# A decay mixer's first batch: gate products in four other PSUM banks, its silu split in two, and its first four decay tiles ahead of the second batch's preparation

## The chip, the cores and the metric

One NeuronCore of a Trainium2 chip runs the whole program. The time is device microseconds (us) for one execution. A core has TensorE (PE) for matrix products, whose weight loads are listed as PEld, VectorE (DVE), ScalarE (ACT), GpSimd (POOL) and the queues that issue DMAs (SP's and POOL's are used here). The engines run each its own list of instructions in order and wait for each other on semaphores. PE writes only to PSUM, which has eight banks of 128 x 512 float32 numbers; ACT and DVE copy its results from there to the on-chip tiles.

## The reference, cut to what matters

The program computes two layers, each of a mixer and a feed-forward part, on x of shape (8, 512, 256), in float32. The change lies in the mixer of the second layer, the decay mixer:

```python
def _L1_attn_ref(x, W_in, conv_w, ln_gamma, ln_beta, W_xproj, A_param, D, W_out):
    xz = x @ W_in                                  # (8, 512, 256) @ (256, 1024)
    xc, z = jnp.split(xz, 2, axis=-1)
    xc = causal_depthwise_conv(xc, conv_w)         # 4 taps
    xc = jax.nn.silu(xc)
    xc = _layernorm(xc, ln_gamma, ln_beta)
    xp = xc @ W_xproj                              # 33 columns
    delta = jnp.clip(jax.nn.softplus(xp[..., :1]), 1e-06, 10.0)
    Bm = xp[..., 1:1 + n]
    Cm = xp[..., 1 + n:]
    A = -jnp.clip(jax.nn.softplus(A_param), 0.1, 10.0)
    decay = jnp.clip(jnp.exp(delta[..., None] * A[None, None]), 1e-06, 1.0)
    y = xc * jnp.einsum('bsn,bsin->bsi', Bm * Cm, decay)
    y = y + xc * D
    return y * jax.nn.silu(z) @ W_out

x = x + _L1_attn_ref(_layernorm(x, axis=-1), ...)
```

## The kernel before

The program has five stages, A to E, and all engines meet at the end of each. The decay mixer is stage D, the class StageD. It takes eight batches of 512 tokens. For each batch there is a preparation, and then 16 units of decay work; the preparation of the next batch is mixed in among the units of the one before.

The preparation of a batch, by step and engine:

- `stats`, `rstd`, `minus`, `norm`: layer norm of x (DVE, ACT, DVE, ACT; line 2016 is the norm).
- `flip` 0 and 1 (PE, line 1906): transposes, evicted by ACT as `flipped`.
- `lift` c (PE, line 1916): product with 128 columns of W_in. c = 0 to 3 are the convolution's half, c = 4 to 7 the gate's. Each is evicted by ACT (line 2004, `lifted`).
- the convolution: two quarters on PE (`conv` 0 and 1, line 1924, evicted as `conved`), two on DVE (`taps` 2 and 3, lines 2129 and 2132).
- `silu` on ACT: a table load, the silu of the convolution (line 2043), the silu of the gate (line 2046), and a table load back (line 2047).
- `turnx` (PE, line 1931), `stats2`, `rstd2`, `xn` (DVE, line 2145): transposes to tokens by channels, and the second layer norm.
- `back` (PE, line 1939), `xf` (ACT, line 2004 with a bias), `xproj` (PE, line 1948): transposes back, and the product with W_xproj.
- `pj`, `soft`, `clip`, `rep`, `scalars` (DVE line 2154, ACT lines 2062 and 2064, DVE, PE line 1957, DVE line 2169): the step sizes and the products Bm * Cm, spread over the partitions. `zx` on POOL multiplies the gate in.

A unit u of decay work covers eight tokens: `grow` u on ACT (line 2074, one exponential over 128 x 2048), `scale` u on DVE (line 2181, four instructions), and a quarter of `sum` on PE (line 1966), which sums four units into one bank. `wout`, `turnw`, `gate`, `proj` and `acc` follow once for four units.

Once per stage come `decay` on ACT (lines 1997 and 1999) and `bound` on DVE (lines 2103 and 2105), which make A, and `consts` and `spread` on DVE.

One written order sets everything. `order()` walks u from -27 and puts down, for each u, `grow` u+2, `scale` u, `sum`, the output steps, and then the pieces of PLAN for each batch, one entry per u. Batch 0 has its own list, START, and batch 1's PLAN starts at u = -10. Each engine runs its own steps of this one list in that order. PE's products of the preparation share a ring of four banks, 4 to 7 (`self.ring`): a step waits until the use four before it was evicted. Banks 0 and 1 take the sums, 2 the transposed sums and 3 the output product; none of them is in use before the first `sum`.

Of the kernel before, what the change touches and what calls it, by code (L numbers as in the profile page):

```python
# [11 lines left out]
ACT = mybir.ActivationFunctionType  # L12
# [5 lines left out]
LN_EXP = "natural_log_exp_and_others"  # L18
# [7 lines left out]
class Arena:  # L26
    def __init__(self, tensor, start, end):
        self.t, self.at, self.end = tensor, start, end
# [171 lines left out]
def act_rstd(e, m, own, sb):  # L200

    s6, mv, r = sb
    e.activation(r, mv[:, :, 1], ACT.Ln, bias=m.eps5).then_inc(*own.tick())
    e.wait_ge(*own.now())
    return e.activation(r, r, ACT.Exp, scale=-0.5)
# [9 lines left out]
def take_stats(ar):  # L215
    return ar.take([4, 6]), ar.take([4, 2]), ar.take([4])
# [801 lines left out]
class StageB:  # L1018
# [137 lines left out]
    def sp(self, e):  # L1156
# [19 lines left out]
        def load(w):  # L1176
            if w >= 2 * NB:
                return
            if w >= 3:
                e.wait_ge(s["st"], 20 * (w - 2))  # L1180
            for which in range(2):
                e.wait_ge(self.d_scr[which], 16 * (w + 1))
                order = (0, 1, 0, 2, 0, 1, 2, 1) if which else (0, 0, 1, 0, 2, 1, 1, 2)
                for row, part in enumerate(order):
                    e.dma_start(self.stacks[which][w % 3][16 * row:16 * row + 16],
                                self.scr[w % 3 + 3 * which][:, part, :].rearrange("(h j) t -> j h t", j=16)).then_inc(
                                    self.d_stack[which][w % 3], 16)
# [596 lines left out]
class StageD:  # L1784
# [6 lines left out]
    def __init__(self, m, c):  # L1791
        self.m, self.c = m, c
        ar = Arena(m.Z, m.LO, m.HI)
        self.gy = [ar.take([256]) for _ in range(4)]
        self.An = ar.take([4, 512])
        self.wout = ar.take([4, 256])
        self.win = ar.take([2, 1024])
        self.wxp = ar.take([4, 33])
        self.rep = ar.take([4, 128])
        self.pick = ar.take([32])  # L1800
        self.diag = ar.take([2, 4, 128])
        self.dcol = ar.take([4])
        self.sb, self.sb2 = take_stats(ar), take_stats(ar)
        self.nb = ar.take([4])
        self.pj = ar.take([4, 33])
        self.src = ar.take([4, 17])
        self.dl = [ar.take([4, 4]) for _ in range(2)]
        self.bc = [ar.take([16, 4]) for _ in range(2)]
        self.nf = ar.take([2, 512])
        self.xp = ar.take([4, 515])  # L1810
        self.nt = ar.take([4, 256])
        self.xc = ar.take([4, 512])
        self.z = ar.take([4, 512])
        self.xn, self.xf = self.xp[:, :, 3:515], self.xc
        self.zx = [ar.take([4, 512]) for _ in range(2)]
        self.e = [ar.take([4, 512]) for _ in range(10)]
        self.wt = [ar.take([512]) for _ in range(2)]
        self.yf = [ar.take([4, 128]) for _ in range(2)]
        self.wb, self.tb, self.ob = m.banks[0:2], m.banks[2], m.banks[3]
        self.steps = self.order()  # L1820
        self.uses = {}
        for step in self.steps:
            if step[0] in ("flip", "lift", "conv", "turnx", "back", "xproj", "rep"):
                self.uses[step] = len(self.uses)
        self.ring = m.ring(m.banks[4:8], len(self.uses))
        self.d_gy = m.landings(0, 4, 32)
        self.s = {n: m.sem("d_" + n) for n in (
            "d_w", "d_a", "added", "pads", "an", "consts", "moments", "rstd", "nb", "nt", "prod", "conv", "gate", "xc",
            "xn", "bc", "raw", "dl", "sc", "zx", "grow", "scale", "sum", "wt", "tw", "yf", "op", "acc")}

    def use(self, *step):
        return self.uses[step]
# [12 lines left out]
        (("scalars",),))  # L1845


    START = (
        (("stats",), ("consts",)), (("rstd",), ("minus",), ("spread",)), (("norm",), ("decay",)), (("flip", 0), ("flip", 1)),
        (("flipped", 0), ("flipped", 1), ("lift", 2)), (("lifted", 2), ("lift", 3)),  # L1850
        (("lifted", 3), ("taps", 2), ("lift", 0)), (("lifted", 0), ("taps", 3), ("lift", 1)), (("bound",),),
        (("lifted", 1), ("conv", 0)), (("conved", 0), ("conv", 1))) + PLAN[10:]

    def order(self):
        N, out = 16 * NB, []
        for u in range(-27, N + 12):
            b, v = divmod(u, 16)
            if u + 2 in range(N):
                out.append(("grow", u + 2))
            if u in range(N):  # L1860
                out.append(("scale", u))
            w, j = divmod(u - 4, 4)
            if w in range(N // 4):
                out.append(("sum", w, j))
            w -= 1
            if w in range(N // 4):
                out += [[("wout", w)], [("turnw", w)], [("gate", w)], [("proj", w)]][j]
            if j == 0 and w - 1 in range(N // 4):
                out.append(("acc", w - 1))
            for x in range(NB):  # L1870
                at = u - 16 * (x - 1) + 10
                if at == -1:
                    out += [("fetch", x), ("add", x)]
                plan = self.PLAN if x else self.START
                if at in range(len(plan)):
                    out += [(s[0], x) + s[1:] for s in plan[at]]
        return out

    def walk(self, **do):
# [14 lines left out]
    def pe(self, e):  # L1894
        m, s, ring, ident = self.m, self.s, self.ring, self.m.ident
        def bank(*step):
            r = self.use(*step)
            if r >= 4:
                e.wait_ge(*ring.done(r - 4))
            return ring.buf(r)  # L1900
# [8 lines left out]
        def lift(b, c):  # L1909
            if b == 0:  # L1910
                e.wait_ge(s["d_w"], 64)
            for kb in range(2):
                e.wait_ge(*ring.done(self.use("flip", b, kb)))
            o = bank("lift", b, c)
            for k in range(2):
                ins = e.matmul(o, self.win[:, k, c * 128:(c + 1) * 128], self.nf[:, k, :], start=k == 0, stop=k == 1)  # L1916
            ins.then_inc(s["prod"], 1)

        def conv(b, c):
            e.wait_ge(s["consts"], 1)  # L1920
            e.wait_ge(*ring.done(self.use("lift", b, c)))
            o = bank("conv", b, c)
            for w in range(4):
                ins = e.matmul(o, self.diag[:, c, w, :], self.xp[:, c, w:w + 512], start=w == 0, stop=w == 3)  # L1924
            ins.then_inc(s["prod"], 1)
# [34 lines left out]
        def sums(w, q):  # L1960
            if q == 0:
                e.wait_ge(s["scale"], 4 * w + 4)
                if w >= 2:
                    e.wait_ge(s["wt"], w - 1)
            for j in range(4):
                ins = e.matmul(self.wb[w % 2][32 * j:32 * j + 32, :], self.pick, self.e[(4 * w + j) % 10][:, q, :],  # L1966
                               start=q == 0, stop=q == 3)
            if q == 3:
                ins.then_inc(s["sum"], 1)
# [9 lines left out]
        def proj(w):  # L1979
# [3 lines left out]
            for k in range(4):  # L1983
                ins = e.matmul(self.ob[:, 0:256], self.yf[w % 2][:, k, :], self.wout[:, k, :], start=k == 0, stop=k == 3)  # L1984
            ins.then_inc(s["op"], 1)

        self.walk(flip=flip, lift=lift, conv=conv, turnx=turnx, back=back, xproj=xproj, rep=rep, sum=sums, turnw=turnw,
                  proj=proj)

    def act(self, e):  # L1990
        m, s, ring, own, vec = self.m, self.s, self.ring, self.m.own["act"], self.m.vec
# [47 lines left out]
        def silu(b):  # L2039
# [6 lines left out]
            e.activation(self.z, self.z, ACT.Silu).then_inc(s["gate"], 1)  # L2046
            e.preload_act_table_set(LN_EXP)

        def rstd2(b):
            e.wait_ge(s["moments"], 2 * b + 2)  # L2050
            act_rstd(e, m, own, self.sb2).then_inc(s["rstd"], 1)
# [24 lines left out]
        def wout(w):  # L2076
            e.wait_ge(s["sum"], w + 1)
            if w >= 2:
                e.wait_ge(s["tw"], w - 1)
            e.activation(self.wt[w % 2], self.wb[w % 2], ACT.Copy).then_inc(s["wt"], 1)  # L2080

        self.walk(decay=decay, rstd=rstd, norm=norm, flipped=flipped, lifted=lifted, conved=conved, silu=silu, rstd2=rstd2, xf=xf,
                  soft=soft, grow=grow, wout=wout)

    def dve(self, e):
# [142 lines left out]
class StageE:  # L2228
# [3 lines left out]

    START = (range(5), ("hidden", 0, 0), range(5, 8), ("hidden", 0, 1), range(8, 15), ("down", 0, 0, 0), ("down", 0, 0, 1),
             ("hidden", 0, 2), range(15, 17), ("hidden", 0, 3), ("hidden", 0, 4), range(17, 18), ("hidden", 0, 5))
# [29 lines left out]
    def order(self):  # L2264
        out = []
        for what in self.START:
            out += [("prep", 0, p) for p in what] if isinstance(what, range) else [what]
# [372 lines left out]
```

## Time and profile before

| what | value |
|---|---|
| time, median of 3 runs | 3248.0 us (3244.1 to 3249.63) |
| the profiled execution: its time | 3243.28 us |
| the profiled execution: its span | 3241.4 us |
| mean granted PE clock, share of full speed | 0.937 |
| busy share of the span: PE, DVE, ACT, POOL | 86%, 66%, 50%, 32% |
| first instruction of stage D on ACT | 2104.32 us |
| first instruction of stage E on ACT | 2687.96 us |

All times inside the execution are counted from the start of the span. A busy time is the time in which an engine worked. The idle time that a row names was spent before the instructions of that row, and the engine and line behind the arrow are what ended it. A PE clock of 1.00 is 2.4 GHz and 0.50 is 1.2 GHz.

### The profile page before, as it was taken

The numbers are of one execution on the slowest core, as the hardware profiler recorded it, in microseconds if no ns is written. First come the engines' busy times: TensorE is split into PE (matmuls) and PEld (weight loads), VectorE is DVE, ScalarE is ACT, GpSimd is POOL, SyncE is SP. The second block draws the span as 40 slices with busy tenths as digits, with TensorE's granted clock in tenths as the row PEclk, the third lists the DMA queues.
The fourth block names the chain that finished last, engine by engine and source line by source line (L and its number), as shares of the span: only waits on it lengthen the run. The fifth ranks groups of instructions, "written<-read, shape, count | busy, mean of one in ns | idle before, by whom it ended". The sixth has DMA issues, their size and how long they took to land.

```text
span 3241.4 us, 40482 instructions
## 1 busy us (share of the span) xinstructions
PE 2788.6 (86%) x13782; PEld 1680.9 (52%) x13782; DVE 2130.8 (66%) x3827; ACT 1629.6 (50%) x2433; POOL 1030.1 (32%) x715
## 2 busy tenths in 40 slices
PE   6878878887765799999969999968888988999999
PEld 3445544554443455555535666534444445666666
DVE  0688898888895677777522222246777785777776
ACT  2778778777861355555431111148877781111111
POOL 0888888888781221121010000011111000110000
PEclk9899999999867899999979999979999998999999
DMA  3577887788773775555432000010000002000000
GB/s 106 118 169 148 179 172 168 147 180 172 161 169 81 192 184 90 93 81 91 54 133 67 23 23 23 19 49 7 7 7 14 1 1 59 7 14 7 7 7 13
DMA packets 119272, 262.94 MB, mean 81 GB/s; under 512 B 14784, under 2 KB 72896, under 8 KB 117408
## 3 DMA queue, kind: packets, MB, share of 16 engines
q0 software_dynamic: 24928, 134.89, 20.0%
q1 hardware_dynamic: 94144, 125.47, 16.9%
q8 instruction: 115, 1.88, 0.2%
q14 instruction: 85, 0.70, 0.1%
HBM read 135.40 MB, written 131.20 MB: 82 GB/s over the span
## 4 chain that ended last, share of the span: by engine, by line
PE 50%; issue 6%; ACT 6%; DVE 5%; DMA 1%; SPq 0%; POOL 0%; POOLq 0%; ACTq 0%; DVEq 0%
PE PS L2345 7%; PE PS L1625 6%; PE PS L2363 6%; PE PS L1916 4%; PE PS L1647 3%; PE PS L1288 2%; PE PS L1966 2%; ACT Z L2074 2%; PE PS L1245 2%; PE PS L1267 2%; PE PS L1924 2%; PE PS L1270 2%; PE PS L1215 2%; PE PS L1984 1%; PE PS L1314 1%
## 5 line engine op out<-in xcount | busy, mean ns | idle before, releaser
L804 POOL TENSOR_TENSOR Z<-Z 128x1024 f32<-128x1024 f32 x256 | 648.4, 2761 | 45.8 <-DMA Z<-rows_b 40.9
L714 DVE TENSOR_TENSOR_SCAN Z<-PS,Z 128x1024 f32<-128x1024 f32 x256 | 576.5, 2276 | 18.4 <-POOL Z L804 13.6
L508 PE MATMUL PS<-Z 128*128 128x128 f32 x2048 | 305.1, 295 | 121.3 <-DVE Z L714 47.6
L508 PEld LDWEIGHTS PS<-Z 128*128 128x128 f32 x2048 | 250.7, 151 | 252.6 <-issue 81.7
L646 ACT ACTIVATE PS<-Z 128x511 f32<-128x511 f32 x512 | 332.8, 688 | 68.2 <-DVE Z L714 67.6
L1384 ACT ACTIVATE Z<-PS 128x512 f32<-128x512 f32 x320 | 188.9, 596 | 266.7 <-PE PS L1270 261.4
L2396 ACT ACTIVATE Z<-PS 128x512 f32<-128x512 f32 x144 | 85.9, 597 | 415.4 <-PE PS L2345 415.4
L2345 PE MATMUL PS<-Z 128*128 128x512 f32 x576 | 275.3, 604 | 7.9 <-DVE Z L2478 7.1
L658 ACT ACTIVATE Z<-PS,Z 128x512 f32<-128x512 f32 x378 | 246.0, 684 | 68.3 <-PE PS L508 61.5
L1477 DVE TENSOR_REDUCE Z<-PS 128x1 f32<-128x512 f32 (+2 forms) x384 | 182.8, 508 | 120.2 <-PE PS L1246 116.6
L2074 ACT ACTIVATE Z<-Z 128x2048 f32<-128x2048 f32 x128 | 252.4, 1996 | 12.9 <-PE PS L1966 9.3
L468 PE MATMUL PS<-Z 128*128 128x512 f32 x512 | 244.6, 607 | 13.6 <-ACT Z L577 12.8
L1625 PE MATMUL PS<-Z 128*128 x560 | 248.9, 598 | 0.6 <-issue 0.6
L2363 PE MATMUL PS<-Z 128*128 128x256 f32 x1024 | 243.0, 380 | 1.8 <-DVE Z L2493 1.8
L2181 DVE TENSOR_SCALAR Z<-Z 128x512 f32<-128x512 f32 x512 | 234.6, 527 | 5.7 <-ACT Z L2074 5.6
L2363 PEld LDWEIGHTS PS<-Z 128*128 128x128 f32 x1024 | 193.6, 190 | 80.3 <-issue 53.6
L2493 DVE SCALAR_TENSOR_TENSOR Z<-PS,Z 128x256 f32<-128x256 f32 x512 | 213.9, 476 | 9.9 <-PE PS L2363 9.9
L2478 DVE TENSOR_TENSOR Z<-Z,PS 128x512 f32<-128x512 f32 x144 | 98.2, 686 | 134.0 <-ACT Z L2396 134.0
L2222 POOL TENSOR_TENSOR Z<-Z 128x512 f32<-128x512 f32 x32 | 44.5, 1422 | 437.5 <-ACT Z L2004 437.5
L1752 DVE TENSOR_TENSOR Z<-Z,PS 128x512 f32<-128x512 f32 x70 | 48.2, 689 | 198.2 <-PE PS L1625 198.2
L1625 PEld LDWEIGHTS PS<-Z 128*128 128x128 f32 x560 | 104.6, 192 | 120.1 <-issue 120.1
L1245 PE MATMUL PS<-Z 128*128 128x512 bf16 (+3 forms) x512 | 137.1, 310 | 29.6 <-issue 13.5
(289 smaller groups left out, 4959.9 us busy)
## 6 DMA issues: line engine op xcount, KB each, us to landing
sums<-Z POOLq DMA_DIRECT2D x112, 768.0 KB, 8.4
Z<-rows_b SPq DMA_DIRECT2D x128, 256.0 KB, 4.6
Z<-scr SPq DMA_DIRECT2D x256, 128.0 KB, 7.2
rows_n<-in_L_ffn_expert_wv POOLq DMA_DIRECT2D x32, 528.0 KB, 7.7
scr<-Z SPq DMA_DIRECT2D x32, 384.0 KB, 3.5
Z<-Z POOLq DMA_DIRECT2D x14, 768.0 KB, 7.6
Z<-in_L_ffn_expert_wv SPq DMA_DIRECT2D x4, 2048.0 KB, 15.0
Z<-sums SPq DMA_DIRECT2D x7, 768.0 KB, 6.3
```

Source lines behind the costliest of these rows:

```text
L468: ins = e.matmul(self.bank("conv", b, c)[0], self.conv[:, w, k, c * 128:(c + 1) * 128], self.n_fm[:, k, w:w + 512], start=i == 0, stop=i == 7)
L508: ins = e.transpose(self.turned[i % 2][:, c * 128:(c + 1) * 128], self.h(k, c // 2)[:, c % 2, i * 128:(i + 1) * 128], ident)
L646: ins = e.activation(self.aa[f][:, c, 1:512], self.de[b % 2][:, 2 * f + c, 1:512], ACT.Exp, scale=self.An[:, q:q + 1])
L658: e.activation(self.pr[k % 3][:, i - 1, :], self.turned[i % 2], ACT.Copy, scale=self.ct[b % 2][:, i, 16 + n:17 + n]).then_inc(s["yprod"], 1)
L714: e.tensor_tensor_scan(h, a, h, 0.0, ALU.mult, ALU.add).then_inc(s["scan"], 1)
L804: e.tensor_tensor(self.h(k, f), self.du[b % 2][:, 2 * f:2 * f + 2, :], b3(self.Bs[k % 2], 1, [128, 2, 512]), ALU.mult).then_inc(s["hin"], 1)
L1625: ins = e.matmul(ub[n], self.hs[c % 2][:, k, :], self.wv[:, bass.ds(expert[c] * 4096 + (2048 * k + 512 * n), 512)], start=k == 0, stop=k == 1)
L2074: e.activation(self.e[u % 10], self.An, ACT.Exp, scale=self.dl[b % 2][:, j, i:i + 1]).then_inc(s["grow"], 1)
L2181: ins = e.tensor_scalar(o, o, 1e-6, self.bc[b % 2][:, 4 * j + i, q:q + 1], ALU.max, ALU.mult)
L2345: ins = e.matmul(self.up[n % 2], w, self.nf[b % 2][:, k, :], start=k == 0, stop=k == 1)
L2363: ins = e.matmul(o[:, j * 256:(j + 1) * 256], self.hd[n % 4][:, c], self.w2[:, x - 1, :], start=True, stop=True)
L2493: ins = e.scalar_tensor_tensor(xx, o[:, j * 256:(j + 1) * 256], self.cw[b % 2][:, t, x - 1:x], xx, ALU.mult, ALU.add)
```

## The change

For batch 0 alone, four things are different:

1. The gate products (`lift` 4 to 7 before, `zlift` 4 to 7 now) go to banks 0 to 3 in place of the ring, with semaphores of their own, `zl` and `zo`. They stand after the convolution: `zlift` 4 before `turnx`, the other three behind it.
2. The silu is in two steps. `silux` is directly behind the last eviction of the convolution. `siluz`, the gate's, is behind `soft`. Each of the two loads its table and loads the other back.
3. `decay` moves from behind `norm` to a place between the last `lifted` and the first `conved`, and `bound` from behind the taps to a place behind `xn`.
4. The steps of batch 0 after the convolution each come several u earlier. `grow` 0 to 3 and `scale` 0 to 3 stand in START's last entry, at u = -6: behind batch 1's `norm` and `flip`, and ahead of its `flipped` evictions. Before, they were at u = -2 to 3, between batch 1's later pieces.

The first `sum` additionally waits for the evictions of the gate products. From `grow` 4 on the order is the one before.

```diff
     START = (
-        (("stats",), ("consts",)), (("rstd",), ("minus",), ("spread",)), (("norm",), ("decay",)), (("flip", 0), ("flip", 1)),
+        (("stats",), ("consts",)), (("rstd",), ("minus",), ("spread",)), (("norm",),), (("flip", 0), ("flip", 1)),
         (("flipped", 0), ("flipped", 1), ("lift", 2)), (("lifted", 2), ("lift", 3)),
-        (("lifted", 3), ("taps", 2), ("lift", 0)), (("lifted", 0), ("taps", 3), ("lift", 1)), (("bound",),),
-        (("lifted", 1), ("conv", 0)), (("conved", 0), ("conv", 1))) + PLAN[10:]
+        (("lifted", 3), ("taps", 2), ("lift", 0)), (("lifted", 0), ("taps", 3), ("lift", 1)),
+        (("lifted", 1), ("conv", 0)), (("decay",), ("conved", 0), ("conv", 1)), (("conved", 1), ("silux",), ("zlift", 4)),
+        (("zlifted", 4), ("turnx", 0), ("turnx", 1), ("turnx", 2), ("turnx", 3)),
+        (("zlift", 5), ("zlift", 6), ("stats2",), ("zlifted", 5), ("zlift", 7)), (("rstd2",), ("zlifted", 6)),
+        (("xn", 0), ("xn", 1), ("xn", 2), ("xn", 3), ("zlifted", 7), ("bound",)),
+        (("back", 0), ("back", 1), ("back", 2), ("back", 3)),
+        (("xf", 0), ("xf", 1), ("xf", 2), ("xf", 3), ("xproj",)), (("pj",), ("soft",)), (("clip",), ("rep",), ("siluz",)),
+        (("zx",), ("scalars",)), tuple(("grow",) for _ in range(4)) + tuple(("scale",) for _ in range(4)))
...
-            if u + 2 in range(N):
+            if u + 2 in range(4, N):
                 out.append(("grow", u + 2))
-            if u in range(N):
+            if u in range(4, N):
                 out.append(("scale", u))
...
+        def zlift(b, c):
+            for k in range(2):
+                ins = e.matmul(m.banks[c - 4], self.win[:, k, c * 128:(c + 1) * 128], self.nf[:, k, :], start=k == 0, stop=k == 1)
+            ins.then_inc(s["zl"], 1)
...
+                if w == 0:
+                    e.wait_ge(s["zo"], 4)
...
+        def zlifted(b, c):
+            e.wait_ge(s["zl"], c - 3)
+            e.activation(self.z[:, c - 4, :], m.banks[c - 4], ACT.Copy).then_inc(s["zo"], 1)
+
+        def silux(b):
+            for c in range(2):
+                e.wait_ge(*ring.done(self.use("conv", b, c)))
+            e.wait_ge(s["conv"], 2)
+            e.activation(self.xc, self.xc, ACT.Silu).then_inc(s["xc"], 1)
+            e.preload_act_table_set(LN_EXP)
+
+        def siluz(b):
+            e.wait_ge(s["zo"], 4)
+            e.activation(self.z, self.z, ACT.Silu).then_inc(s["gate"], 1)
+            e.preload_act_table_set(LN_EXP)
```

## Rows read from the trace of the kernel before

**Rows 1.** Stretches of stage D: length, busy of each engine, PE clock, DMA share, GB/s.
```profile
2102.00:2182.00 80.00, 45.93 (x153) 27.62 (x153) 28.65 (x75) 30.84 (x45) 17.02 (x17) 0.72 0.20 55
2182.00:2220.00 38.00, 29.64 (x118) 13.81 (x116) 27.39 (x74) 37.16 (x33) 0.00 (x0) 0.82 0.00 1
2220.00:2280.00 60.00, 54.40 (x285) 25.34 (x284) 39.98 (x112) 44.93 (x44) 10.69 (x8) 1.00 0.03 10
```

**Rows 2.** The chain that ended last: start, length, what; x16 are 16 half passes.
```profile
2127.77 9.88 PE PS L1916 x16
2137.65 6.87 PE PS L1924 x16
2144.52 6.88 PE PS L1916 x16
```

**Rows 3.** PE's timeline: start, length, line, idle before and its releaser.
```profile
2122.97 1.94 PE L1906 MATMUL PS<-Z 128*128 128x128 f32 x8 [20.88 <-ACT Z L2016]
2155.30 3.68 PE L1931 MATMUL PS<-Z 128*128 128x128 f32 x16 [3.91 <-ACT Z L2043]
2170.54 2.07 PE L1916 MATMUL PS<-Z 128*128 128x512 f32 x4
2172.45 3.66 PE L1948 MATMUL PS<-Z 128*128 128x33 f32 x32
2196.15 1.92 PE L1966 MATMUL PS<-Z 128*32 128x512 f32 x16
2269.73 1.97 PE L1931 MATMUL PS<-Z 128*128 128x128 f32 x16 [1.53 <-ACT Z L2043]
```

**Rows 4.** ACT's timeline in the preparation of batch 0.
```profile
2122.73 1.90 ACT L1997 ACTIVATE Z<-Z 128x2048 f32<-128x2048 f32 x1
2126.56 1.07 ACT L2004 ACTIVATE Z<-PS 128x512 f32<-128x512 f32 x2
2152.04 1.28 ACT L2043 ACT_TABLE_LOAD   x1
2153.34 1.91 ACT L2043 ACTIVATE Z<-Z 128x2048 f32<-128x2048 f32 x1
2162.49 0.28 ACT L203 ACTIVATE Z<-Z 128x4 f32<-128x4 f32 x1
2163.24 2.07 ACT L2016 ACTIVATE Z<-Z 128x256 f32<-128x256 f32 x4 [0.23 <-DVE Z L2120]
2168.23 3.34 ACT L2004 ACTIVATE Z<-PS,Z 128x512 f32<-128x512 f32 x4 [0.26 <-PE PS L1939]
2176.71 0.30 ACT L2064 ACTIVATE Z<-Z 128x4 f32<-128x4 f32 x1
```

**Rows 5.** DVE's timeline in the preparation of batch 0.
```profile
2159.11 2.49 DVE L192 BATCH_NORM_STATS2 Z<-PS 128x6 f32<-128x512 f32 x4 [15.72 <-PE PS L1931]
2163.12 2.96 DVE L2145 TENSOR_SCALAR Z<-PS,Z 128x512 f32<-128x512 f32 x4
2176.14 0.30 DVE L2154 COPY Z<-PS 128x132 f32<-128x132 f32 x1 [10.06 <-PE PS L1948]
```

**Rows 6.** ACT's timeline from the first decay tile to behind batch 1's silu.
```profile
2182.40 2.00 ACT L2074 ACTIVATE Z<-Z 128x2048 f32<-128x2048 f32 x1 [2.09 <-DVE Z L2169]
2196.60 0.60 ACT L2004 ACTIVATE Z<-PS 128x512 f32<-128x512 f32 x1
2198.97 0.60 ACT L2004 ACTIVATE Z<-PS 128x512 f32<-128x512 f32 x1
2199.59 1.28 ACT L2043 ACT_TABLE_LOAD   x1
2205.91 5.79 ACT L2074 ACTIVATE Z<-Z 128x2048 f32<-128x2048 f32 x3
```

**Rows 7.** Single microseconds: PE busy, granted PE clock, DMA share, GB/s.
```profile
2153.00:2154.00 1.00, 0.00 (x0) 0.92 0.00 0
2283.00:2284.00 1.00, 0.00 (x0) 0.77 0.00 0
```

More of the change, by code:

```diff
@@ L1828, in __init__ @@
             "d_w", "d_a", "added", "pads", "an", "consts", "moments", "rstd", "nb", "nt", "prod", "conv", "gate", "xc",
-            "xn", "bc", "raw", "dl", "sc", "zx", "grow", "scale", "sum", "wt", "tw", "yf", "op", "acc")}
+            "xn", "bc", "raw", "dl", "sc", "zx", "grow", "scale", "sum", "wt", "tw", "yf", "op", "acc", "zl", "zo")}
     def use(self, *step):
@@ L1875, in order @@
                 if at in range(len(plan)):
-                    out += [(s[0], x) + s[1:] for s in plan[at]]
+                    pieces = [(s[0], x) + s[1:] for s in plan[at]]
+                    out += [(s[0], n % 4) if s[0] in ("grow", "scale") else s for n, s in enumerate(pieces)]
         return out
@@ L1985, in proj @@
             ins.then_inc(s["op"], 1)
-        self.walk(flip=flip, lift=lift, conv=conv, turnx=turnx, back=back, xproj=xproj, rep=rep, sum=sums, turnw=turnw,
+        self.walk(flip=flip, lift=lift, zlift=zlift, conv=conv, turnx=turnx, back=back, xproj=xproj, rep=rep, sum=sums, turnw=turnw,
                   proj=proj)
@@ L2080, in wout @@
             e.activation(self.wt[w % 2], self.wb[w % 2], ACT.Copy).then_inc(s["wt"], 1)
-        self.walk(decay=decay, rstd=rstd, norm=norm, flipped=flipped, lifted=lifted, conved=conved, silu=silu, rstd2=rstd2, xf=xf,
+        self.walk(decay=decay, rstd=rstd, norm=norm, flipped=flipped, lifted=lifted, conved=conved, silu=silu, zlifted=zlifted, silux=silux, siluz=siluz, rstd2=rstd2, xf=xf,
                   soft=soft, grow=grow, wout=wout)
```

## The prediction, as it was put on record before the result was known

> **What bounds the kernel now.** I first read the busy time by stretches of stage D. The reader is to see three regimes [rows 1]: until 2182 no engine is full (PE 46 of 80 us), so the first preparation is a chain of single steps; from 2182 to 2220 ACT is full (37.2 of 38 us); from 2220 on PE leads with 54.4 of 60, ACT has 44.9 and DVE 40.0. Then the chain of work that ended last: in the first regime it is three blocks on PE, the four convolution lifts (9.88 us), the convolution (6.87) and the four gate lifts (6.88) [rows 2]. Only then comes batch 0's silu. The timelines of PE, ACT and DVE give what stands between them, and the single microseconds give PE's clock.
>
> Everything behind batch 1's silu is the same list of steps in both kernels. At that silu the same units have been grown and the same sums are outstanding. So the change is worth what it does to the start of batch 1's silu, whose table load begins at 2199.59 [rows 6]. I work the new timeline out to that point.
>
> **Lifts of batch 0.** `decay` leaves the place ahead of `flipped`. Before, it began at 2122.73 and the two evictions ended at 2127.63 [rows 4]. The second flip ends at 2124.91 [rows 3], so now they end about 2125.6 and the lifts begin at 2125.7, 2.1 us earlier. With 9.88 and 6.87 us [rows 2] the convolution ends at 2142.4. `decay`, about 3.8 us from its start to the eviction behind it [rows 4], now lies on ACT from 2136.2 to 2140.1 while PE computes the convolution. It holds `conved` 0 up by about 1 us, but the silu waits for `conved` 1, ready at 2142.4; that cover is worth the 3.8 us. `bound` (2.4 us) runs on DVE while PE and ACT do `back` and `xf`.
>
> **Silu and turns.** `conved` 1 ends at 2143.0. Before, the load started at 2152.04 and `turnx` at 2155.30 [rows 3, 4], 3.26 later; so `turnx` starts at 2146.3. That is 9.0 earlier: the 2.1, and the gate lifts' 6.88. `zlift` 4 fills 1.7 of PE's 3.9 us. Does the clock fall in the other 2.2? When PE had stood still from 2151.4, the clock fell only within 2153:2154 (0.92 there [rows 7]). And after 1.53 us of rest a `turnx` took 1.97 us, against 3.68 for batch 0's at half clock [rows 3]. I take 1.97, which ends at 2148.3; 3.68 stays as the bound.
>
> **From the turns to the step sizes.** From the end of `turnx` (2158.98) to the start of `xn` there were 4.1 us [rows 3, 5], of which 0.5 were batch 1's `rstd`, done ahead; without it 3.65. `xn` takes 2.96 [rows 5] and ends at 2154.95. `zlift` 5 to 7 take 5.15 (three quarters of 6.88) and end at 2153.45; their evictions fit into ACT's gaps. `back` starts at 2155.05, and ACT's four `xf` at 2155.75, lasting 3.34 [rows 4]: 2159.1. `xproj` follows at once, without the lift that stood ahead of it, for 3.5 to the next step; from `pj` to the end of `soft` 2176.14 to 2177.01 is 0.87 [rows 4, 5]. `soft` ends at 2163.6. It ended at 2177.0, so batch 0 is 13.4 us ahead here. Before, the step sizes then waited for DVE's taps 2 and 3 of batch 1, and the first tile came at 2182.40 [rows 6].
>
> **What now stands ahead of batch 1.** ACT's order is now `soft`, batch 1's `rstd`, `siluz`, batch 1's `norm`, `grow` 0 to 3, and only then batch 1's `flipped`. `rstd` takes 0.5 (two such instructions [rows 4]), to 2164.1. `siluz` is a load, a silu and a load back: 1.30 + 1.91 + 1.28 = 4.5 [rows 4], to 2168.6. `norm` 2.07: 2170.65. Before it began at 2163.24 [rows 4], now 5.3 us later. `clip`, `rep` and `scalars` are done by 2167.5 behind this cover. Four `grow` at 1.93 (5.79 for three [rows 6]) are 7.7: 2178.4. PE has flipped batch 1 by 2172.7 and waits. Two evictions 1.07 [rows 4]: 2179.45. PE's lifts of batch 1 begin at 2179.55, where they began at 2170.54 [rows 3]: 9.0 later. That is the price of the early tiles: the 9.0 us won in front of `turnx` are spent on a second table pair and on four tiles that hold the evictions back.
>
> **The rest of batch 1.** PE had rested for nearly 7 us, so the lifts run as batch 0's did: 9.88, then 6.87 and 6.88 [rows 2]. They end at 2203.2; before, with batch 0's `xproj` and `rep` in between, they ended when the first sum began, at 2196.15 [rows 3]. That is +7.0 on PE. On ACT: the first gate lift can be evicted at 2198.05; each following pair of decay and eviction takes 2.37 (2196.60 to 2198.97 [rows 6]), three pairs 7.1, the last eviction 0.6. The table load of batch 1's silu starts at 2205.8, which is **+6.2 us**. ACT was 2.8 us late behind PE there and is still 2 us late; the full stretch of ACT is eased by hardly 1 us, because `grow` 4 to 6 still stand between the same evictions. ACT rests meanwhile, from 2180 to 2198, but for six evictions.
>
> Behind it the same steps follow with the same waits. The profiled execution's 3243.3 us become 3249.5. Its own time lies 4.7 under the median, so the median of 3248.0 becomes **3254.2**.
>
> ACT's page in the Trainium skill bears on the split silu. This trace shows a load of 1.28 us and the silu 1.30 after the load's start [rows 4], so the added pair costs 2.6, all of it inside `siluz`. "ScalarE: Activation LUTs", under "What ACT_TABLE_LOAD costs", puts a switch at 1.28 plus a drain of 1.38, and under "Table sets" advises doing all of one set before switching, which speaks against a split. By its price the two loads on the path would add 2.8 more and the time would be an estimated 3257; the rows show no such drain, and I go by them.
>
> **Bounds.** The batch 0 lifts follow the flips after 0.8 us of rest where it was 2.9; if they run at full clock throughout they take 6.88, 3.0 less. The same holds for batch 1's, although 7 us of rest speak against it. If the clock has fallen by `turnx`, the turns take 1.7 more, the three gate lifts twice 5.15, so that `back` waits for them 3.5 more, and `back` and `xproj` perhaps 1.3 more: +6.5. In low use the clock did fall once with rests of about 2 us (0.77 in 2283:2284 [rows 7]).
>
> **Rivals.**
> - *The first preparation runs at half clock* (+6.5): +12.7, 3260.7. For it: rests of 1.6 to 2.2 us follow each other from 2144 on. Against: batch 2's `turnx` after such a rest. It decides if PE's clock is below 1.00 before `turnx` starts.
> - *The lifts run at full clock* (-3.0 once or twice): +3.2 or +0.2, 3251 or 3248. For it: the shorter rest. Against: both sets begin after the clock was at 0.50.
> - *ACT is the bound, and the tiles taken out of its full stretch are a gain*: 7.7 us of decay leave 2182:2220, where ACT is 98% busy [rows 1], the rest lying under that cover: 3248.0 - 7.7 = 3240.3. This ends on the other side. It needs batch 1's lifts not to be late. From their start the table load follows in 26.3 us (9.88 + 6.87 + 1.8 + 7.1 + 0.6), so it turns into a gain when they start before 2173.3, and reaches 7.7 only if they start before 2165.6. Against it: ACT runs in order, and the four tiles stand ahead of `flipped`; PE leads from 2220 on.
> - *Nothing is passed on*, because the regime from 2220 on has slack: 3248. Against it: PE runs in order at 91% there and cannot catch up.
>
> **How the numbers follow.** What a measurement can tell here is about 0.2%, 6.5 us: above 3254.5 is slower, under 3241.5 faster. My forecast 0.58, own range 3251 to 3258, half of it on either side of the bound; half clock in front 0.14; full clock in the lifts 0.11; nothing passed on 0.04; ACT as the bound, or a similar gain, 0.13. Slower is 0.29 + 0.14 and 0.01 of others, 0.44; same is 0.29 + 0.11 + 0.03, 0.43; faster 0.13. The range reaches from 3246, which holds the full-clock case, to 3261, which holds the half-clock case; the gain is left out.
>
> **What would show it.** `turnx` of batch 0 at 2146.3 with a length near 2.0; its `soft` ending near 2163.6; two table loads around a single silu before batch 1's norm; the first `grow` near 2170.7 (11.8 earlier); PE resting some 7 us before batch 1's first lift at 2179.5, with clock 0.50; the load of batch 1's silu at 2205.8. Stage E would start at 2694. The prediction fails if the evictions of batch 1's flips are not behind the four tiles, if the clock takes another course in front, or if the time from one batch's silu to the next changes behind batch 1.

## The result, and the profile after

The changed kernel takes 3257.0 us (median of 20 runs, 3250.7 to 3268.7), the kernel before in the same measurement 3250.6 (20 runs, 3241.8 to 3260.1). The ratio is 1.0027 with a 95% interval of 1.0014 to 1.0039: slower by some 9 us, with 4.5 to 12.7 in the interval. The difference of the medians is 6.4. The forecast was +6.2.

The two profiled executions differ by more, 3251.8 against 3241.4 us of span. Stage D's first table load on ACT stands at 2108.87 where it was 2104.32, and batch 0's norm at 2125.78 where it was 2120.75. So 5.0 of the 10.4 us arose ahead of anything that was changed. I therefore count from batch 0's norm: to the table load of batch 1's silu it was 78.84 us before and is 84.17 now, to stage E's first table load 567.21 and 572.51. Both grew by 5.3.

ACT's timeline of the changed kernel, from `soft` to the evictions of batch 1's flips, and the table load of batch 1's silu (start, length, line, idle before):

```profile
2168.82 0.30 ACT L2095 ACTIVATE Z<-Z 128x4 f32<-128x4 f32 x1
2169.02 0.28 ACT L203 ACTIVATE Z<-Z 128x4 f32<-128x4 f32 x1
...
2169.56 1.28 ACT L2077 ACT_TABLE_LOAD   x1
2170.85 1.91 ACT L2077 ACTIVATE Z<-Z 128x2048 f32<-128x2048 f32 x1
2172.78 1.28 ACT L2078 ACT_TABLE_LOAD   x1
2174.08 2.07 ACT L2031 ACTIVATE Z<-Z 128x256 f32<-128x256 f32 x4
2176.06 7.67 ACT L2105 ACTIVATE Z<-Z 128x2048 f32<-128x2048 f32 x4
2183.63 1.05 ACT L2019 ACTIVATE Z<-PS 128x512 f32<-128x512 f32 x2
...
2209.95 1.28 ACT L2058 ACT_TABLE_LOAD   x1
```

The reader is to see that ACT has no rest here: the gate's silu with its two loads, the norm, then 7.6 us of four tiles between 2176.1 and 2183.6, and only then the two short evictions. PE's timeline shows who waits for them; it answers to [rows 3].

```profile
2130.72 10.16 PE L1924 MATMUL PS<-Z 128*128 128x512 f32 x16 [0.78 <-ACT Z L2019]
2151.71 1.97 PE L1944 MATMUL PS<-Z 128*128 128x128 f32 x16 [2.24 <-ACT Z L2072]
2164.25 3.96 PE L1961 MATMUL PS<-Z 128*128 128x33 f32 x32 [1.76 <-ACT Z L2019]
2176.20 1.97 PE L1914 MATMUL PS<-Z 128*128 128x128 f32 x8 [4.33 <-ACT Z L2031]
2184.78 8.74 PE L1924 MATMUL PS<-Z 128*128 128x512 f32 x16 [6.61 <-ACT Z L2019]
2207.18 1.92 PE L1981 MATMUL PS<-Z 128*32 128x512 f32 x16
```

PE flips batch 1 at 2176.2, rests 6.61 us until ACT (line 2019, the evictions) lets it go, and begins the lifts at 2184.78. The chain that ended last goes the same way (start, length, what):

```profile
2169.56 1.28 ACT L2077
...
2170.85 1.91 ACT Z L2077
...
2176.15 7.57 ACT Z L2105 x4
2183.72 0.49 ACT Z L2019
2184.21 0.57 issue
2184.78 8.74 PE PS L1924 x16
2193.52 6.87 PE PS L1937 x16
```

The four tiles (line 2105) and the gate's silu, both beside PE's work before, are now on the chain.

### The profile page after: what moved, and what is told of

It is laid out like the page before. It is cut to its first block, busy times and chain, and to the rows that moved or that the text cites. A ratio compares the mean times of both kernels' runs of the same rounds, so it can differ in the third digit from the quotient of the medians.

```text
span 3251.8 us, 40475 instructions
## 1 busy us (share of the span) xinstructions
PE 2786.2 (86%) x13782; PEld 1678.6 (52%) x13782; DVE 2131.0 (66%) x3827; ACT 1631.3 (50%) x2435; POOL 1029.7 (32%) x715
## 4 chain that ended last, share of the span: by engine, by line
PE 50%; issue 6%; ACT 6%; DVE 5%; DMA 1%; SPq 0%; POOL 0%; POOLq 0%; ACTq 0%; DVEq 0%
PE PS L2376 7%; PE PS L1625 6%; PE PS L2394 6%; PE PS L1924 3%; PE PS L1647 3%; PE PS L1288 2%; ACT Z L2105 2%; PE PS L1981 2%; PE PS L1245 2%; PE PS L1267 2%; PE PS L1937 2%; PE PS L1270 2%; PE PS L1215 2%; PE PS L1999 1%; PE PS L1314 1%
## 5 line engine op out<-in xcount | busy, mean ns | idle before, releaser
L2212 DVE TENSOR_SCALAR Z<-Z 128x512 f32<-128x512 f32 x512 | 234.8, 528 | 16.9 <-ACT Z L2105 16.6
```

What stands on the lines that cost most here:

```text
L2212: ins = e.tensor_scalar(o, o, 1e-6, self.bc[b % 2][:, 4 * j + i, q:q + 1], ALU.max, ALU.mult)
```

## The experiments

Every kernel is read by three distances from batch 0's norm on ACT: to PE's first lift of batch 1, to the table load of batch 1's silu, and to stage E's first table load. The column behind them is the third less the second. "Again" is a further execution of an unchanged kernel. Distances are those of one profiled execution each; the ratios rest on 5 to 20 runs. The diffs show only the parts of lines that changed.

| kernel | lifts of batch 1 | silu of batch 1 | stage E | silu to stage E | ratio to before, 95% interval |
|---|---|---|---|---|---|
| before | 49.8 | 78.8 | 567.2 | 488.4 | 1 |
| before, again | 47.9 | 77.2 | 565.6 | 488.4 | |
| changed | 59.0 | 84.2 | 572.5 | 488.3 | 1.0027 (1.0014 to 1.0039) |
| changed, again | 60.6 | 85.7 | 574.0 | 488.3 | 1.0023 (1.0002 to 1.0043) |
| decay moved alone | 47.8 | 76.9 | 565.2 | 488.4 | 1.0003 (0.9987 to 1.0018) |
| tiles behind the evictions | 54.7 | 81.1 | 573.7 | 492.6 | 1.0014 (0.9997 to 1.0032) |
| tiles at their old places | 55.0 | 81.4 | 572.6 | 491.2 | 1.0023 (1.0009 to 1.0037) |
| one more table pair | 61.6 | 87.1 | 585.8 | 498.6 | 1.0053 (1.0031 to 1.0074) |
| gate's silu moved alone | 55.1 | 80.5 | 577.2 | 496.7 | 1.0008 (0.9996 to 1.0021) |
| silu and tiles beside the lifts | 50.6 | 76.5 | 569.3 | 492.8 | 0.9993 (0.9978 to 1.0009) |
| the same, with filler on PE | 48.1 | 75.7 | 568.5 | 492.9 | 0.9989 (0.9970 to 1.0009) |
| filler in PE's rest | 59.0 | 84.1 | 572.5 | 488.3 | 1.0047 (1.0031 to 1.0064) |

The distance to stage E does not hold all of it. From stage E's first table load to the end of the execution it takes 553.4 to 553.5 us in the six executions that have 488.3 to 488.4 in the last but one column, 552.0 or 552.1 in four of the other six, 548.7 with the gate's silu moved alone and 553.7 with one more table pair. So where the way to stage E was longer, the way from there was mostly shorter. The granted clock over stage E's first 50 us was 0.73 in both kernels and with one more table pair, 0.76 with silu and tiles beside the lifts and 0.86 with the gate's silu moved alone. From batch 0's norm to the end the kernel before takes 1120.6 and 1119.0 us, the changed kernel 1126.0 and 1127.6, the gate's silu moved alone 1125.9, silu and tiles beside the lifts 1121.3, and the same with filler 1120.6.

**Decay moved alone**, in the kernel before:

```diff
-(("norm",), ("decay",)), (("flip", 0), ("flip", 1)),
+(("norm",),), (("flip", 0), ("flip", 1)),
...
-(("bound",),), (("lifted", 1), ("conv", 0)), (("conved", 0), ("conv", 1))
+(), (("lifted", 1), ("conv", 0)), (("decay",), ("bound",), ("conved", 0), ("conv", 1))
```

> The kernel before with one part of the change alone: decay behind the last lift's eviction, bound behind it. I read each run by the distance from batch 0's norm on ACT to the table load of batch 1's silu (before 78.8 us, the changed kernel 84.2) and to stage E's table load (before 567.2, changed 572.5). My theory, single steps one after the other: the first lifts start 2.1 us after the flips' end instead of 2.9 later, every step to batch 1's silu moves by the same 2.1, so 76.7 and 565.1. Rival, the wait goes elsewhere (the clock rises at the same moment, or another step ends last): 78.8 and 567.2. The time itself (1 us in 1600) can't be told from no change.

The silu of batch 1 and stage E both come 2.0 us earlier than in the first profile of before. PE's rest in front of the first lifts fell from 2.87 to 0.78 us and nothing takes its place, as the theory said. Seen against the other profile of before it is 0.3 and 0.4, so the size rests on the two having the same clock in front (first lifts 9.88 and 9.94 us, `turnx` 3.68 in both; 9.11 and 2.60 in the other profile); the start of the first lifts, from 7.0 to 4.9 us behind the norm, does not depend on it.

**Tiles behind the evictions**, in the changed kernel:

```diff
-(("zx",), ("scalars",)), tuple(("grow",) for _ in range(4)) + tuple(("scale",) for _ in range(4))
+(("zx",), ("scalars",)), (), tuple(("grow",) for _ in range(4)) + tuple(("scale",) for _ in range(4))
```

> The changed kernel with grow and scale 0 to 3 one place later, behind the evictions of batch 1's flips. Theory of the prediction (the four tiles hold the evictions and so PE's lifts back): the lifts of batch 1 start right behind the flips, 5.9 us earlier than in the changed kernel; the tiles run on ACT beside the four lifts; distance to batch 1's silu 78.3, to stage E 566.6, the time that of before (ratio 1.000). Rival 1, the loss comes from the split silu or the clock and not from the tiles: 84.2 and 572.5, ratio 1.002 to 1.003. Rival 2, ACT's full stretch was the bound and the early tiles are now a net gain: 76 or less.

The rest in front of the lifts fell from 6.61 to 0.73 us, so the tiles did hold PE back.

```profile
2178.64 1.97 PE L1914 MATMUL PS<-Z 128*128 128x128 f32 x8 [4.34 <-ACT Z L2031]
2181.34 9.98 PE L1924 MATMUL PS<-Z 128*128 128x512 f32 x16 [0.73 <-issue]
```

The distance to the silu became 81.1, not 78.3. In this execution the clock fell in front: `turnx` took 2.46 and `xproj` 5.57 us, where the changed kernel's profile has 1.97 and 3.96. Against the second profile of the changed kernel, with nearly the same front (`xproj` 5.59), the tiles' share is 4.6 us (85.7 to 81.1), smaller than 5.9 because the lifts took 9.98 at low clock in place of 8.74. Rival 1 is out as the whole story, rival 2 too. The time itself (1.0014) cannot be told from the changed kernel's.

**Tiles at their old places**: START ends with `(("zx",), ("scalars",))`, and `grow` and `scale` run over all of `range(N)`.

> The changed kernel with grow and scale 0 to 3 back at their old places among batch 1's pieces; the banks and the split silu stay. Theory of the prediction: PE as in the kernel with the tiles behind the evictions (lifts at the same place), but ACT is again 3.4 us late behind the last gate lift where it was 2.6 late, so 79.1 to batch 1's silu and 567.4 to stage E, as before the change. The early chain by itself is worth nothing, since the second table pair and the silu of the gate stand ahead of batch 1's norm. Rival, the early front does pay and only the tiles cost: 73 to 75.

The lifts start 0.3 us behind those of the run above, and the silu comes at 81.4, against 81.1 there and 79.1 expected: the clock was low in front again (`turnx` 3.02, `xproj` 6.30 us), and the lifts of batch 1 took 9.22. The rival's 73 to 75 did not come: the 9 us won ahead of `turnx` do not reach batch 1. The early tiles are worth a little once they are out of the way. The 0.3 us between the two silus hides it, because the lifts above took 9.98 us; from the start of the convolution to the silu it was 16.6 us with the early tiles and 17.3 without, 0.7 less, where 0.8 were expected.

**One more table pair** ahead of the gate's silu:

```diff
             e.wait_ge(s["zo"], 4)
+            e.preload_act_table_set(EXTRA)
+            e.preload_act_table_set(LN_EXP)
             e.activation(self.z, self.z, ACT.Silu).then_inc(s["gate"], 1)
```

`EXTRA` names another table set.

> The changed kernel with one more pair of table loads (another set, and back) ahead of the gate's silu: the suspected cost doubled. Theory of the prediction, a load is 1.29 us and on the path: batch 1's norm 2.6 later, distance to batch 1's silu 86.8, to stage E 575.1. By a switch's price with a drain: 89.5 and 577.8. Rival, the loads lie beside other work: 84.2 and 572.5.

PE's flips of batch 1 move from 50.42 to 53.00 us behind the norm, by 2.58: two loads of 1.29, and all of it on the path. The silu moves by 3.0, since the lifts took 9.12 in place of 8.74. The Trainium skill, "ScalarE: Activation LUTs", "What ACT_TABLE_LOAD costs", gives a switch 1.38 us more for a drain; two switches would by that have been an estimated 5.3, and the trace does not agree. Its advice under "Table sets", to do all of one set before switching, held: the split put a pair on the path. Stage E, at 585.8, is 13.3 later than in the changed kernel, of which the front explains 3.0.

**Gate's silu moved alone**, behind the evictions, the tiles left ahead of them:

```diff
-(("clip",), ("rep",), ("siluz",)),
+(("clip",), ("rep",)),
-(("zx",), ("scalars",)), tuple(("grow",) for _ in range(4)) + tuple(("scale",) for _ in range(4))
+(("zx",), ("scalars",)), tuple(("grow",) for _ in range(4)) + tuple(("scale",) for _ in range(4)), (("siluz",),)
```

> The changed kernel with the gate's silu (4.5 us with its two table loads) moved behind the evictions of batch 1's flips, and the four tiles left ahead of them. Theory: the silu then lies beside PE's lifts, the norm and everything behind it start 4.5 us earlier, so the lifts of batch 1 at 54.5 us and its silu at 79.7 behind batch 0's norm (changed kernel 59.0 and 84.2; 1 or 2 more if the clock falls in front). With the run in which the tiles alone stand behind the evictions (54.7 and 81.1) this gives both halves of the price. Rival, the silu beside the lifts holds the first eviction and so the convolution back: 82 to 84. Behind batch 1's silu 488.3 to 493 to stage E.

The front is that of the changed kernel's first profile to 0.1 us. The lifts start 3.9 us earlier (59.0 to 55.1), not 4.5: the first tile now waits for the step sizes, since the norm ends ahead of `rep`, which took 1.95 us at low clock. The silu comes 3.7 earlier. This is the other half of the price. Behind batch 1's silu, though, the way to stage E took 8.4 us more than in the changed kernel's profile. Single stretches of PE show where (PE busy, PE clock, DMA share, GB/s), and PE's timeline what ran in them:

```profile
2220.00:2226.00 6.00, 3.08 (x25) 0.98 0.00 0
2226.00:2230.00 4.00, 4.00 (x19) 0.50 0.00 0
2230.00:2236.00 6.00, 6.00 (x27) 0.50 0.21 56
2236.00:2242.00 6.00, 6.00 (x21) 0.71 0.11 36
```

```profile
2224.95 1.59 PE L1914 MATMUL PS<-Z 128*128 128x128 f32 x8 [1.94 <-ACT Z L2019]
2226.46 1.94 PE L1981 MATMUL PS<-Z 128*32 128x512 f32 x8
2228.33 7.04 PE L1961 MATMUL PS<-Z 128*128 128x33 f32 x32
```

The reader is to see a PE that is busy all the time from 2226 to 2242 and is granted 0.50 (1.2 GHz) for 10 us and more of it, after a stretch in which it was busy for only half the time at 0.98. Batch 1's `xproj` took 7.04 us where before it took 3.76 (at 2223.71). The run with one more table pair has the same 7.04, and in these two the granted clock was 0.84 over the 75 us behind batch 1's silu, against 0.91 in the profiles of before and changed. The time does not bear the 8.4 out as the price of this edit: the ratio is 1.0008, below the changed kernel's, and from batch 0's norm to the end this execution took 1125.9 us, the changed kernel's 1126.0.

**Silu and tiles beside the lifts.** From what these runs said I put all of it where PE computes: the gate's silu and two tiles behind the evictions, two tiles ahead of `conved` 0, tile 4 ahead of `conved` 1.

```diff
-(("clip",), ("rep",), ("siluz",)),
+(("clip",), ("rep",)),
-(("zx",), ("scalars",)), tuple(("grow",) for _ in range(4)) + tuple(("scale",) for _ in range(4))
+(("zx",), ("scalars",)), (), (("siluz",), ("grow", 0), ("grow", 1), ("scale", 0), ("scale", 1)), (), (), (),
+(("grow", 2), ("grow", 3), ("scale", 2), ("scale", 3)), (("grow", 4),)
```

In `order()`, `grow` then starts at 5 in the loop, since tile 4 stands in START.

> The changed kernel with the gate's silu behind the evictions of batch 1's flips, tiles 0 and 1 behind it, tiles 2 and 3 ahead of the first eviction of batch 1's convolution, tile 4 ahead of the second. Theory of the prediction (what stands on ACT between the step sizes and batch 1's lifts is the whole price): lifts of batch 1 start about 48.8 us after batch 0's norm (59.0 in the changed kernel), distance to batch 1's silu 75.0 at full clock in front, up to 77 when the clock falls there as in two runs before; before 78.8. Time 2 to 4 us under before, ratio 0.999. Rival 1, ACT cannot do the silu and five tiles beside the lifts: 78 to 80. Rival 2, the course of the clock behind batch 1's silu decides more than this: the ratio lies at 1.000 or above although the distance to the silu is shorter.

The silu of batch 1 comes at 76.5, as expected with a low clock in front: 7.7 to 9.2 us before the changed kernel's two profiles and 0.7 to 2.4 before those of before. The time does not show it against before (0.9993, with 1 inside the interval). The way to stage E took 4.4 us more than before, and the way from there to the end 1.4 to 1.5 less; norm to end is 1121.3 us, no less than the 1120.6 and 1119.0 of before.

**The same, with filler on PE**: pairs of products of 128 x 512 into bank 3, which nothing reads, ahead of `turnx`, `xproj` and `rep`.

```diff
+        def fill(b, n):
+            if n != 2:
+                e.wait_ge(s["zo"], 4)
+            for _ in range(n % 10):
+                e.matmul(m.banks[3], ident, self.wout[:, 0:2, :].rearrange(FLAT), start=True, stop=True)
```

> The kernel with the gate's silu beside the lifts, and six products of 128 x 512 more on PE whose results nothing reads, two each in its pauses ahead of turnx, xproj and rep. If the low clock of the front comes from these pauses, the clock stays at 1.00 from the lifts of batch 0 to those of batch 1, which take 6.9 us in place of 9 to 10; distance to batch 1's silu 72 to 73. If the clock falls all the same, each pair takes 3.4 us where there is 1.7 to 2.2 of room, and the distance is 77 to 79.

The expectation came true in part. PE's timeline (line 1944 is the filler, 1967 `xproj`, 1924 the lifts, 1937 the convolution):

```profile
2162.39 1.88 PE L1944 MATMUL PS<-Z 128*128 128x512 f32 x4
2164.32 4.04 PE L1967 MATMUL PS<-Z 128*128 128x33 f32 x32
2168.17 3.36 PE L1944 MATMUL PS<-Z 128*128 128x512 f32 x4
...
2174.03 7.10 PE L1924 MATMUL PS<-Z 128*128 128x512 f32 x16 [0.78 <-ACT Z L2025]
2183.92 8.80 PE L1937 MATMUL PS<-Z 128*128 128x512 f32 x16 [2.78 <-ACT Z L2025]
```

The lifts of batch 1 took 7.10 us in place of 9.82, and every execution of the changed kernel and its other variants took 8.70 to 9.98 for them. The clock did dip once: the pair ahead of `rep` took 3.36. Behind that pair `rep` took 1.00 us and the flips 1.04, against 1.95 and 1.97 in all of those. The two pairs ahead of `turnx` and `xproj` are not shown to do anything: those steps took 1.97 and 4.04, as they do in unfilled executions whose first lifts took about as long as the 10.08 here (see `turnx` below). So part of the gain at the lifts' start, 50.6 to 48.1, is the front's own clock. But the gain ends at the next wait: ACT is still at the silu and the tiles, PE rests 2.78 us in front of the convolution, and that then runs partly at low clock, 8.80. The silu comes at 75.7, 0.8 earlier than without filler.

**Filler in PE's rest** of the changed kernel: three such products between the flips and the lifts of batch 1.

> The changed kernel with three products of 128 x 512, which nothing reads, in PE's rest of 6.6 us between batch 1's flips and its lifts. Theory: the half clock of the lifts comes from that rest and costs 1.9 us there (8.7 in place of 6.9); with PE busy before them the lifts take 6.9 to 7.1, still starting at 59.0, and batch 1's silu comes at 82.3. Rival, the products run at half clock and the clock rises no earlier: lifts 8.7, silu at 84.2.

The lifts took 8.70, the silu came at 84.1. These are the rival's numbers, but not its reason, since the clock did rise. The single stretches show why (columns as above):

```profile
2177.00:2179.00 2.00, 2.00 (x5) 0.50 0.12 25
2179.00:2181.00 2.00, 2.00 (x5) 0.67 0.33 107
2181.00:2183.00 2.00, 0.43 (x2) 1.00 0.23 66
2183.00:2184.00 1.00, 0.09 (x1) 0.86 0.47 131
2184.00:2186.00 2.00, 2.00 (x3) 0.50 0.00 0
```

The products did bring the clock up, to 1.00 by 2181. They ended at 2181.4, and in the 2.5 us of rest that were left the clock fell again, just ahead of the lifts. So whether filler over the whole rest would win the 1.9 us was not tried. The time of this kernel, 1.0047, lies above the changed kernel's although its profile has the same three distances; the two intervals overlap between 1.0031 and 1.0039, and I have no cause to offer for the rest.

**Both kernels again.**

> The changed kernel, once more. Theory: the front is the same, batch 1's silu 84.2 us behind batch 0's norm with 1 or 2 us of the clock's play. Stage E's table load was 572.5 behind the norm; two experiments had 3 to 6 us more than their front explains, with a low clock on a fully busy PE. If that play belongs to each execution and not to those edits, this run of an unchanged kernel may show it too: 570 to 580.

> The kernel before, once more, one look. Distance to batch 1's silu 78.8; to stage E's load 567.2 if the clock takes the same course, up to 6 more if the play belongs to each execution.

The distance from the silu to stage E repeats within 0.1 us in both, 488.3 and 488.4. The play is in front: before, the first lifts took 9.11 and `turnx` 2.60 us, against 9.88 and 3.68 in the first profile [rows 2, 3]; changed, 9.24 and 2.48 against 10.16 and 1.97, and `xproj` 5.59 against 3.96. So the two pairs of profiles give the change +5.3 and +8.6 at batch 1's silu, 6.9 in the mean. Stage D itself began at 2112.5 (before again) and 2122.3 (changed again) where the first profiles had 2104.3 and 2108.9: up to 18 us of play between executions arise ahead of stage D, in code that no kernel here changes, and in these four profiled executions that makes up most of the spread, since stage E's first load to the end is 553.4 to 553.5 us in all of them. The runs without a profile, which spread as much, cannot be taken apart.

## Why the prediction was right, point by point

- *What bounds the front.* Right. It is a chain of single steps and each edit passed through it at its own size: 2.0 for `decay`, 2.6 for a table pair, 3.9 for the silu moved off, 5.9 for the tiles moved off (at PE's first lift of batch 1).
- *Lifts of batch 0* 2.1 earlier: they start 4.94 behind the norm in place of 7.02. They took 10.16 us in place of 9.88; the shorter rest ahead of them did not bring the clock up sooner. In the nine executions with the changed kernel's front they took 8.67 to 10.17 and never 6.88, so the full-clock rival is out here.
- *`turnx`* was to start 25.6 behind the norm (2146.3 less 2120.75) with 1.97 us; it started at 25.9 and took 1.97. Of the eight executions with this front and no filler ahead of `turnx`, four had 1.97 and four 2.46 to 3.02, so this was an even choice, and that the first profile has 1.97 is luck. The two kinds can be told by the first lifts: where these took 10.12 to 10.17 us, `turnx` took 1.97 and `xproj` 3.96 to 3.99; where they took 8.67 to 9.26, so that the clock had risen earlier, `turnx` took 2.46 to 3.02 and `xproj` 5.57 to 6.30. The rests between are the same 2.24 us in both. What sets the clock's moment in the lifts stays open. The half-clock rival came true in part in the changed kernel's second profile, at +1.6 in place of +6.5, as the clock fell later than that rival had it.
- *`soft` ending* 42.85 behind the norm: 43.3. Inside it two misses cancelled: `xf` took 2.79 in place of 3.34, and `xproj` to the next step 4.0 in place of 3.5, as the clock fell within it (0.65 over 2167:2169). Two table loads around one silu, 4.5 us: 4.50. First tile at 49.9: 50.3. PE's rest of nearly 7: 6.61. First lift of batch 1 at 58.8: 59.0.
- *The rest of batch 1.* The term that was mis-sized is the lifts' 9.88; they took 8.74, since the clock rose earlier (by 2188:2190 it was 0.98). The convolution and the gate lifts were as shown before, and so were the 2.4 us a pair of tile and eviction. Batch 1's silu came at 84.2 where 85.0 was forecast (+5.3 in place of +6.2). The second pair of profiles has +8.6 there, so that +6.2 lies between the two is partly luck too.
- *Behind it the same waits.* Right for this change, to 0.1 us in both profiles. As a rule it failed: six of the experiments took 3 to 10 us more from that silu to stage E, with the same steps behind it. It went mostly in two places. Between the silus of batch 1 and batch 2, all executions of before and changed took 66.9 us; it was 68.5 with silu and tiles beside the lifts, with and without filler, 70.1 with the tiles behind the evictions, 73.3 with the gate's silu moved alone and 73.4 with one more table pair. Between batch 7's silu and stage E it was 80.7 before and changed, and 83.5 to 83.6 in five of the six. In the stretch that I opened, it went to a low clock on a busy PE.
- *ACT as the bound.* Refuted: with the tiles early and out of the way, the way from the convolution to the silu was 0.7 us shorter than with the tiles at their old places, not 7.7. *Nothing passed on*: refuted, since stage E came 5.3 and 8.5 us later in the two pairs of profiles.
- *The bound of 1.3 for `back` and `xproj` at half clock* was too narrow: `xproj` alone took up to 6.3 in these fronts, and 7.0 elsewhere, in place of 3.7.

The version with the silu and the tiles beside the lifts undoes the loss, but neither it nor its filler variant is shown to beat the kernel before.

## What to carry to other kernels

Work that is brought forward on an engine that runs in order is paid for by what stands behind it there. Look for the short step that another engine waits for (here two evictions of 0.5 us) and put the long ones behind it. A chain of single steps can be added up from a trace to within a microsecond, as long as the clock takes the course that was assumed. What comes behind it repeats only as long as the clock takes the same course, so a difference of a few us needs many runs, and a distance inside the trace that leaves out the play of the other stages. Check that distance against the one to the end of the execution: part of what one stage seems to lose can come back in the next.

## What the runs showed of the hardware that was not expected

- TensorE's clock can be low while the engine is fully busy: 0.50 for 10 us and more in the run with the gate's silu moved alone, from 2226 on, behind 6 us in which PE was busy for 3.1.
- The same kernel in two executions had another clock in front: `xproj` took 3.96 and 5.59 us. The Trainium skill, "TensorE: Matmul & The Clock Gate", Part 1, calls the point of the switch run-variable, and these rows agree.
- `xproj`, 32 passes of only 33 columns, doubled with the half clock (3.66 to 7.04). Each pass loads 128 x 128 weights, and the median load took 192 ns at a clock of 1.00 and 333 ns at 0.50.
- The clock fell from 1.00 to 0.50 within the 2.5 us of rest behind 4.3 us of filler (2181.4 to 2184, filler in PE's rest).
- From batch 1's silu to stage E, six executions of four kernels took 488.3 to 488.4 us, whenever stage D began; six other kernels, in one execution each, took 491.2 to 498.6. What chooses between them stays open.
